# Attention stage of an embedding, attention and feed-forward kernel: small products on 32 rows, a second buffer for x, and another order of each engine's work

## The reference, cut to what matters

```
h = concat(image_patches @ W + b, layernorm(sum of text tables))      # 64 x 93 rows of 192
x = layernorm(h)
w = (x @ w_qkv) split into 12 heads of 64                             # 768 columns
w_normed = w / max(sqrt(sum(w*w over rows)), 1e-12)
Pi = softmax over the rows of (sum(w_normed*w_normed over 64) * temp)
dots = sum over rows of (Pi / (sum(Pi) + 1e-8)) * w*w
h = h + (-(w * Pi) * 1/(1 + dots)) @ w_out + b_out
y = layernorm(h);  z = y @ P                                          # 8 groups of 16
scores = z @ C (8 groups of 64 codes);  top 4 of each group, softmax -> gates
hidden = gelu(z @ W1[code] + b1);  code = sum over the 4 of gate * (hidden @ W2[code] + b2)
out = h + gelu(code @ G1 + g1b) @ G2 + g2b
```

## Time and profile before

| | |
|---|---|
| time, three runs | 1387.41, 1391.74, 1393.82 us (median 1391.74) |
| profiled execution | 1385.12 us, of which 1383.4 us from the first to the last instruction |
| stage 1 | to about 117 us |
| stage 2 | about 117 to 618 us |
| stage 3 | about 618 us to the end |
| granted TensorE clock over the span | 0.956 of full speed |

### The profile page before, as it was taken

One profiled execution on the slowest core, in us unless ns is written; L12 is line 12 of the kernel. 1 busy time (PEld: TensorE's weight loads), 2 busy tenths in 40 slices (PEclk: granted clock), 3 DMA queues, 4 the chain that ended last, 5 costly groups with the idle time before them and its releaser, 6 DMA issues.

```text
span 1383.4 us, 34221 instructions
## 1 busy us (share of the span) xinstructions
PE 1228.8 (89%) x12232; PEld 625.2 (45%) x12232; DVE 1101.5 (80%) x3370; ACT 1086.2 (79%) x2696; POOL 998.8 (72%) x713
## 2 busy tenths in 40 slices
PE   2943799999999999868999999999999999999996
PEld 2942566666666666523343333333343333333332
DVE  5682488888888888957888888888888888888884
ACT  0243467777777667549999999999999999999994
POOL 7741367656775676637888888788888888888884
PEclk7975899999999999969999999999999999999998
DMA  9663312222322222143313322232413223232410
GB/s 274 161 133 74 60 49 84 67 67 74 99 65 68 73 94 67 51 114 88 71 44 86 68 59 65 57 76 53 97 46 90 64 58 65 57 81 51 95 39 12
DMA packets 95705, 107.06 MB, mean 77 GB/s; under 512 B 12772, under 2 KB 92668, under 8 KB 95254
## 3 DMA queue, kind: packets, MB, share of 16 engines
q1 hardware_dynamic: 86576, 94.95, 26.3%
q10 hardware_dynamic: 6848, 6.13, 2.6%
q0 software_dynamic: 2112, 3.79, 1.1%
HBM read 67.88 MB, written 33.71 MB: 73 GB/s over the span
## 4 chain that ended last, share of the span: by engine, by line
PE 21%; ACT 19%; DVE 13%; issue 3%; POOL 1%; SPq 1%; DMA 0%; POOLq 0%; DVEq 0%
ACT ring L1025 12%; DVE arena L1488 11%; PE ring L1741 9%; PE code L1775 9%; ACT arena L1037 6%; PE ring L1794 2%; PE ring L1785 1%; DVE arena L1496 0%; PE code L1662 0%; DMA gate_scales<-arena 0%; ACT arena L1033 0%; POOL arena L764 0%; SPq L611 0%; DVE arena L1273 0%; POOL arena L772 0%
## 5 line engine op out<-in xcount | busy, mean ns | idle before, releaser
L1488 DVE TENSOR_TENSOR arena<-ring,arena 128x496 f32<-128x496 f32 x1008 | 611.8, 668 | 123.4 <-ACT ring L1025 118.7
L827 POOL TENSOR_TENSOR arena<-arena 128x992 f32<-128x992 f32 x264 | 611.5, 2329 | 121.4 <-ACT arena L1037 111.5
L1025 ACT ACTIVATE ring<-ring 128x496 f32<-128x496 f32 x1008 | 544.5, 686 | 18.6 <-PE ring L1741 18.6
L1741 PE MATMUL ring<-arena,w_stack 99*32 99x496 bf16 x6144 | 424.9, 376 | 24.9 <-DVE arena L1488 18.0
L1775 PE MATMUL code<-arena,w_pad 128*32 128x496 f32 x3072 | 389.5, 580 | 8.3 <-DVE arena L1496 8.0
L1741 PEld LDWEIGHTS ring<-arena,w_stack 99*32 99x32 bf16 x6144 | 163.5, 95 | 400.9 <-DVE arena L1488 220.0
L1037 ACT ACTIVATE arena<-ring 128x992 f32<-128x992 f32 x252 | 283.4, 1125 | 0.8 <-PE ring L1741 0.7
L1592 PE MATMUL ring<-arena 96*128 96x372 f32 x384 | 136.3, 493 | 1.8 <-ACT arena L939 0.9
L1775 PEld LDWEIGHTS code<-arena,w_pad 128*32 128x32 f32 x3072 | 97.5, 110 | 59.7 <-DVE arena L1488 22.5
L764 POOL TENSOR_TENSOR arena<-arena 128x372 f32<-128x372 f32 x96 | 91.7, 986 | 32.9 <-DVE arena L1330 32.7
L1592 PEld LDWEIGHTS ring<-arena 96*128 96x128 f32 x384 | 72.1, 195 | 62.9 <-ACT arena L947 15.7
(11 more groups left out here) (143 smaller groups left out, 1418.1 us busy)
## 6 DMA issues: line engine op xcount, KB each, us to landing
arena<-gates SPq DMA_DIRECT2D x48, 496.0 KB, 6.6
gates<-arena SPq DMA_DIRECT2D x16, 744.0 KB, 11.5
arena<-h_scratch SPq DMA_DIRECT2D x32, 279.0 KB
arena<-z_parts SPq DMA_DIRECT2D x144, 62.0 KB, 2.6
h_scratch<-arena SPq DMA_DIRECT2D x16, 279.0 KB
z_parts<-arena SPq DMA_DIRECT2D x48, 93.0 KB, 2.1
arena<-h_scratch SPq DMA_DIRECT2D x12, 372.0 KB
out_h<-arena SPq DMA_DIRECT2D x12, 372.0 KB
```

Of the source, the lines that this page charges most:

```text
L827: p_.tensor_tensor(spaces[quad % SPACES][:, j:j + 2], hid[:, POOL_DUOS.index(duo) % 2], gst[:, block // EB, j:j + 2], ALU.mult).then_inc(s ...
L1025: a_.activation(product, product, ACT.Gelu_apprx_tanh).then_inc(s_hid, 1)
L1488: v_.tensor_tensor(spaces[quad % SPACES][:, j + p], duo_bank(duo, p), gst[:, block // EB, j + p], ALU.mult).then_inc(s_gat, 1)
L1741: mm = t_.matmul(bank[32 * q:32 * q + 32], w1s[:, x + 32 * q:x + 32 * q + 32], zst[:, o, j + p], start=True, stop=True)
```

## The change

The attention stage is rewritten in its products, its buffers and its order. The other two stages keep their instructions, but for the first three `hidden` products and gelus of stage 3, which were placed inside the end of stage 2 and now come after it.

- **Spread.** `pis`, `pi_placed` and `pi_scale_placed` go. Pi stays in `pix` (128 rows, 94 columns), and each `spread_pi(u, c)` is four products with 32 rows each, one for each sequence, into four PSUM banks (0 to 3), at column 94 (c % 5).
- **Scores.** Each of three `scores` is four products with 32 rows and 128 columns, into the same four banks, instead of one with 128 rows and 512 columns.
- **w products** go round four banks instead of two.
- **Head weights** are one operation instead of four.
- **Mean term.** DVE's `mean_term` becomes two POOL operations (the mean negated, then a product with the reciprocal deviation).
- **x.** `x0` has two buffers; after the first two units ACT issues the load (its own queue), instead of SP.
- **Order.** All five passes are written anew; the oldest unit in a pass is now `u4`, and there are one or two more passes.

```diff
-        x0 = c2(ST, [SUB, D])
-        pi = c2(128, [N])
-        pis = c2(128, [UB, N + 1])
+        pix = c2(128, [N + 1])
+        x0 = c2(ST, [2, SUB, D])
...
             def rstd(k, u, eps):
                 wait_apart(pool, (s_mv[k], u + 1), (s_xn[k], u))
+                p_.tensor_scalar_mul(nm[k], mv[k][:, :, 0], -1.0).then_inc(s_nmean[k], 1)
                 p_.tensor_scalar_add(ve[k], mv[k][:, :, 1], eps).then_inc(s_ve[k], 1)
...
+            def mean_term(k, u):
+                pool.wait_ge(s_nmean[k], u + 1)
+                pool.wait_ge(s_rs[k], u + 1)
+                p_.tensor_tensor(nb[k], nm[k], rs[k], ALU.mult).then_inc(s_nb[k], 1)
...
+            def load_x0(u):
+                act.wait_ge(s_xn["A"], u - 1)
+                act.dma_start(x0[:, u % 2], h0_u[u]).then_inc(s_x0[u % 2], 16)
...
             def head_weights(u):
                 dve.wait_ge(s_inv, u + 1)
-                for b in range(UB):
-                    last = v_.tensor_tensor(lsel[:, b, :, 0:HEADS], maskh,
-                                            inv[:, :, b:b + 1].to_broadcast([128, CH, HEADS]), ALU.mult)
-                last.then_inc(s_L, 1)
+                v_.tensor_tensor(lsel[:, :, :, 0:HEADS], maskh.unsqueeze(1).to_broadcast([128, UB, CH, HEADS]),
+                                 inv.rearrange("p c b -> p b c").unsqueeze(3).to_broadcast([128, UB, CH, HEADS]),
+                                 ALU.mult).then_inc(s_L, 1)
...
             def w_pi(u, c):
-                dve.wait_ge(s_pb, CH * u + c + 1)
-                pb = pair0[:, c % 2, 0:UB * (N + 1)].rearrange("p (b n) -> p b n", b=UB)
+                dve.wait_ge(s_pb, CH * u + (5 if c < 5 else 6))
+                x = (N + 1) * (c % 5)
+                pb = ring[:, 0:UB, x:x + N + 1]
...
             def w_product(u, c):
                 if c == 0:
                     pe.wait_ge(s_xt_["A"], u + 1)
-                if c < 2:
-                    wait(pe, s_rsc, CH * (u - 1) + 5 + c)
-                else:
-                    wait(pe, s_wsq, CH * u + c - 1)
-                o = pair0[:, c % 2, 0:UT]
+                if c == 0:
+                    wait(pe, s_rsc, CH * u)
+                if c >= 4:
+                    wait(pe, s_wsq, CH * u + c - 3)
+                o = ring[:, c % 4, 0:UT]
...
             def scores(u, s):
                 if s == 0:
                     pe.wait_ge(s_zf, u + 1)
-                    pe.wait_ge(s_h1, 2 * (u + 1))
-                wait(pe, s_sc, SUB * u + s)
-                t_.matmul(banks[2][0:ST, :], zf[:, ST * s:ST * s + ST], cbd, start=True, stop=True).then_inc(s_sp, 1)
+                    wait(pe, s_wsq, min(CH * (u + 3), CH * UNITS))
+                    wait(pe, s_rsc, min(CH * (u + 2), CH * UNITS))
+                for j in range(PAIRS):
+                    rows = slice(32 * j, 32 * j + 32)
+                    last = t_.matmul(ring[0:ST, j, 128 * s:128 * s + 128], zf[rows, ST * s:ST * s + ST],
+                                     cbd[rows, 128 * j:128 * j + 128], start=True, stop=True)
+                last.then_inc(s_sp, 1)
...
             def spread_pi(u, c):
                 pe.wait_ge(s_pix, u + 1)
-                pe.wait_ge(s_pip, u + 1)
-                if c < 2:
-                    pe.wait_ge(s_wsq, CH * u + 5 + c)
-                else:
-                    wait(pe, s_rsc, CH * u + c - 1)
-                t_.matmul(pair0[:, c % 2, 0:UB * (N + 1)], headsel[:, c], pis.rearrange("p b n -> p (b n)"),
-                          start=True, stop=True).then_inc(s_pb, 1)
+                if c == 0:
+                    pe.wait_ge(s_wsq, CH * (u + 1))
+                    wait(pe, s_sc, SUB * (u - 1))
+                if c == 5:
+                    pe.wait_ge(s_rsc, CH * u + 5)
+                x = (N + 1) * (c % 5)
+                for b in range(UB):
+                    rows = slice(32 * b, 32 * b + 32)
+                    last = t_.matmul(ring[:, b, x:x + N + 1], headsel[rows, c], pix[rows], start=True, stop=True)
+                last.then_inc(s_pb, 1)
...
-                        if not first or duo > 2:
-                            hidden(tile, duo)
+                        hidden(tile, duo)
```

More of the change, by code:

```diff
@@ L374, in build @@
         s_c2d = sem("attention_constants_dve")
-        s_x0, s_xr, s_xb = sem("x0_loaded"), sem("residual_loaded"), sem("residual_biased")
+        s_x0 = [sem(f"x0_loaded_{k}") for k in range(2)]
+        s_xr, s_xb = sem("residual_loaded"), sem("residual_biased")
         s_st = {k: sem(f"stats_{k}") for k in "AG"}
@@ L781, in pass_pool @@
                 if has(u1):
-                    attended(u1, 0)
-                    attended(u1, 1)
                     attended(u1, 2)
-                if has(u2):
-                    shift(u2, 0)
-                if has(u1):
                     attended(u1, 3)
@@ L806, in pass_pool @@
                 if has(u2):
-                    z_part3(u2)
-                if has(n2):
-                    rstd("A", n2, EPS_LN)
+                    shift(u2, 2)
+                if has(u0):
+                    attended(u0, 0)
+                    attended(u0, 1)
             pool.wait_ge(s_w2l, 16 * (6 + UB + S))
@@ L1108, in tile_act @@
             def tile_act(tile, first):
-                for duo in range(3 if first else 0, DUOS):
+                for duo in range(DUOS):
                     gelu(tile, duo)
@@ L1231, in _ @@
             dve.wait_ge(s_zero, 1)
-            for b in range(UB):
-                v_.memset(unitsel[32 * b:32 * b + 32, b:b + 1], 1.0)
             v_.memset(sc[:, :, :, M:M + 8], SENTINEL)
```

441 lines of the change are left out of this document (209 added, 232 removed).

## The result

The changed kernel takes 1396.62 us in the median of 18 runs (1391.05 to 1403.65), the kernel before, run beside it, 1389.60 (18 runs, 1384.56 to 1394.45). The ratio is 1.0065 with a 95% interval of 1.0047 to 1.0082: slower by 0.65%. The profiled execution took 1394.11 us, its span is 1392.3 us (before 1383.4), and the granted TensorE clock over the span is 0.932 (before 0.956). Among the 18 runs the six over 1400 us are those with the lowest clock, 0.926 to 0.929; in the others it is 0.930 to 0.935.

A forecast was written before the change was run, and what follows sets the result against it. No engine is full; a loop across DVE, POOL, ACT and PE sets the pass. 14 passes at -0.68 make -9.5, x -4.2, the end +1.5: -12.2 us from 1391.74, say 1379 us; 8 in 10 between 1358 and 1406.

The forecast's parts named there:

- full granted clock: TensorE clock read in the attention stage before the change, passes of 28.10 us; all forecast terms were priced at it.
- a fall of the clock: Listed sign of being wrong: PE's clock falls below full in the attention stage; no size or chance given.
- The end of the stage: Last units: POOL 2 us late, hidden products moved 1 us, shorter scores 1.5 us less; together +1.5 us.
- The loop: Chain from one norms_floored to the next through DVE, POOL and ACT: 27.5 us a pass, 0.68 less than before.
- the one called the second: Loop through norm "G" on ACT, the first w product and six w copies, ending at 27.8 us.
- the first loop: DVE to residual, POOL's norm and six w2_pi, shift, scores_exp, four w copies: 27.8 us, or 27.1 with norms_floored undisturbed.
- Products on 32 rows: Five spreads on PE take 1.05 us at the logits' price for column pieces, hidden before DVE's first w_pi.
- The rival of serial loads: Spread products on 32 rows run one after another: five spreads 4.2 us, passes 30.7, 1424 us; chance 0.10.
- the first of the two rules: Skill page: a weight load costs its columns at 1.2 GHz, whatever its rows; 40 spread loads about 4.3 us.
- The gates' store: Rival: ACT's next gate copies wait for the store's landing; 5.7 us is harmless, 11.5 gives 1452 us; chance 0.10.
- x in two buffers: Removes the wait for the second x in the first pass, -4.23 us; later passes hardly have it.

The follow-up runs named there:

- the two edits in one kernel: Memsets moved behind the last unit's mean term and bias stores issued before stage 3's loads, added to the fitted-products kernel (93 columns, three gaps): 1378.56 us, ratio 0.9938.
- the stores first: Changed kernel with SP storing bias codes and scales of the last unit but one before the loads for tile 0's second half: 1391.63 us, ratio 1.0037.

## Why the prediction was wrong

It forecast 1379 us against a median of 1391.74, that is -12.2 us. The median came out 7.0 us above that of the kernel before, the span of the profiled execution 8.9. The difference of 21 us, by the profile, lies in two places.

**The clock (13.6 us) is the step that failed.** The prediction read "full granted clock" in the earlier trace rows and priced every term at it. It named a fall of the clock among the things that would make it wrong, but gave it neither a price nor a chance. Yet the change takes work off PE, and the loop still makes it wait: PE's busy time falls from 26.83 of 28.10 us to 22.92 of 27.45. The full clock of before stood beside a PE that rested 1.27 us of a pass; with 4.5 us of rest, 2.45 of it in three neighbouring waits, it was gone in stretches of seven of the 13 passes, and with these three filled it was back. On this the Trainium skill's page "TensorE: Matmul & The Clock Gate", Part 1, says that the low clock is the default and that activity releases it. The trace agrees: 1.00 in the earlier trace rows, 0.89 to 0.94 in the changed kernel's slow passes, 1.00 again with products that nobody reads.

**The end of the stage (+1.5 forecast, +9.2 measured)** was mis-sized. The prediction followed the mean term to POOL, but not past what stands ahead of it there for the last unit, two memsets in `rstd` (5.0 us by the run that moved them, 4.5 of it ahead of stage 3's first gelu). It did not follow SP's order past the loads for stage 3 (2.8 us). Together 7.8; the two edits in one kernel gave 8.1 (834.3 to 826.2). The other 1.6 us, against 824.6 before, were not taken apart; the wait of 3.21 us for the gates' store is still in it. They are also no more than the scatter: from the first gelu of stage 3 to the end the span takes 760.5 to 763.1 us in the changed kernel and its variants, which have the same instructions there.

**The loop was right in size.** Forecast 27.5, measured 27.45 at full clock. By its pieces in the pass from 332.86: DVE to the second half of `residual` (ends 344.00) 11.1 for 11.6; POOL to its first product 3.5 for 3.3 with the handover; six products and a mean term 5.8 for 6.0; the mean term itself 0.20 for 0.3. But the loop that binds is the one called the second: `norm` "G" starts 14.74 us after `norms_floored` (14.9 forecast), and from there it takes 12.71 (12.9). It was added up to 27.8, and came out at 27.45. The 27.5 was the middle of two sums of the first loop, 27.1 and 27.8, which differ by whether `norms_floored` takes 0.18 or 0.87 us; it takes 0.18, and the other loop binds, so that so close a hit is partly luck. POOL's `shift` is done 0.3 us before ACT could use it.

**Products on 32 rows overlap.** Five spreads took 1.37 us, near the 1.05 taken and far from 4.2; DVE's first `w_pi` does not wait. The timeline of PE's weight loads for them:

```profile
343.20 1.21 PEld L1634 LDWEIGHTS ring<-arena 32*128 32x128 f32 x40 [0.86 <-DVE arena L1306]
```

Forty loads, of 185 ns each in the mean, are through in 1.21 us, so they run side by side. The rival of serial loads is out, and with it the first of the two rules that the prediction weighed, taken alone. The Trainium skill's page "TensorE: Matmul & The Clock Gate", Part 3, says that loads to different row groups overlap with running products; the trace agrees. But the 1.05 us came of another price than the one that holds: in the trace four loads start about 7 ns apart and the next four 0.11 us after them, so a group of four costs what the prediction had for one load (0.105 us). Ten groups are 1.05 us as well, by luck.

**The gates' store** lands in 3.6 us in the median, less than the 5.7 taken. ACT's wait at the second group of gate copies is 5.1 us, near the 5.7 forecast, but it is for the bias product on PE: the store was issued at 339.8 us and had landed by 343.5, and the copies start at 345.47. `norm` "G" behind them waits for POOL. That rival is out as well.

**x in two buffers** was forecast at -4.2 us, and in the profiled execution unit 2 came 4.4 us earlier. That near a hit is luck in part: with the memsets moved or the stores first, the same program up to there, unit 2 came at 189.3 and 192.7 us, 3.1 us earlier and 0.3 later than before. The run with one buffer shows that x does more: without it DVE stands 4.1 us in each pass of the new order, and the one pass at full clock takes 29.4 us and not 27.45.

Sum by these terms: 13 passes at -0.73 are -9.5, the start -4.4, the clock +13.6, the end +9.2: +8.9 us.

## What to carry to other kernels

Where a change takes work off TensorE but leaves its waits, price the clock: read how busy the engine was in the passes whose full clock you assume, list its waits in the new order, and look for those that stand close together; here work that fits into them cost nothing and took 14 us off 13 passes, 10 us off the median. Where an operation moves to another engine, read what stands ahead of it there in the first and the last turn of the loop too, not only in the steady one. A part that brings little by the trace of before, such as the second buffer of x, can be what another part of the change rests on.

## What was not expected of the hardware

The clock fell although in these passes no single wait of TensorE is longer than 1.56 us, all but one at most 1.29, and although it was busy 22.92 of the 27.45 us of a full-clock pass. Nine added products in two waits of 1.28 and 0.63 us did not help, eleven in three neighbouring waits of 0.66, 0.52 and 1.27 us did, at nearly the same busy time in a pass. In the changed kernel passes 6 to 8 and 12 to 14 stayed at full clock and passes 2 to 5 and 9 to 11 did not, with the same instructions, and so it was in the runs with the memsets moved and with the stores first; what tells these passes apart is left open.
